# Graph layers on one core: x by V formed ahead of its signs, an identity product ahead of w, stores in another order

## The reference

```
L0: h = relu(batchnorm((A_hat x) W1' + b1)); out = batchnorm(h W2' + b2)
L1: L_norm = D^-1/2 (D - adj) D^-1/2;  _, U = eigh(L_norm)
    agg = U' x;  h = relu(agg W1 + b1);  out = U (h W2 + b2)
L2: graph attention over 256 edges, 4 heads, softmax by source node
L3: two graph convolutions, then LSTMs over windows of 1, 2, 3, 4 nodes
```

## Time and profile before

| | |
|---|---|
| median of 3 runs | 983.21 us (983.03 to 986.38) |
| profiled execution, its time | 983.05 us |
| its span in the trace | 981.2 us |
| TensorE busy | 900.8 us, 92%, 4041 matmuls |
| VectorE busy | 609.9 us, 62% |
| ScalarE busy | 609.8 us, 62% |
| GpSimd busy | 162.3 us, 17% |
| chain that ended last | PE 71%, DVE 16%, ACT 8%, issue 3% |

### The profile page before, as it was taken

How to read it: one execution, slowest core, us unless ns; L and a number is a source line. 1 busy time by engine, 2 the same in 40 slices (tenths; PEclk the granted TensorE clock), 3 DMA queues, 4 the chain that set the end, 5 groups by cost and what they waited for, 6 DMA issues and landing times.

```text
span 981.2 us, 13503 instructions
## 1 busy us (share of the span) xinstructions
PE 900.8 (92%) x4041; PEld 577.1 (59%) x4041; DVE 609.9 (62%) x2143; ACT 609.8 (62%) x1540; POOL 162.3 (17%) x458
## 2 busy tenths in 40 slices
PE   6999968788789987999999999999999999999994
PEld 4565555455566655677776777874444566644442
DVE  6677766657678864666468984335444444444686
ACT  4656647747368862686553456349767788865556
POOL 2334334324333330000000000000000000000065
PEclk9999969979789997999999999999999999999998
DMA  9200000000000000000000000000000000000014
GB/s 268 56 1 1 1 2 1 1 1 2 0 2 1 1 1 1 1 1 1 1 1 1 1 1 1 1 1 1 1 0 1 0 1 1 0 1 0 1 43 129
DMA packets 14329, 13.01 MB, mean 13 GB/s; under 512 B 896, under 2 KB 11056, under 8 KB 14256
## 3 DMA queue, kind: packets, MB, share of 16 engines
q1 hardware_dynamic: 14018, 11.98, 4.4%
q10 hardware_dynamic: 238, 0.16, 0.1%
HBM read 7.89 MB, written 4.19 MB: 12 GB/s over the span
## 4 chain that ended last, share of the span: by engine, by line
PE 71%; DVE 16%; ACT 8%; issue 3%; POOL 1%; DMA 0%; DVEq 0%; ACTq 0%; POOLq 0%
PE bank L982 18%; PE bank L1006 9%; PE bank L844 3%; PE bank L901 3%; PE bank L891 3%; PE bank L834 2%; PE bank L645 2%; PE bank L644 2%; PE bank L573 2%; PE bank L525 2%; PE bank L809 2%; PE bank L969 2%; PE bank L909 2%; PE bank L961 2%; PE bank L798 1%
## 5 line engine op out<-in xcount | busy, mean ns | idle before, releaser
L1489 ACT ACTIVATE hid_t<-bank,gate_b 128x512 f32<-128x512 f32 (+1 forms) x252 | 149.1, 632 | 48.8 <-PE bank L1006 48.2
L1600 POOL TENSOR_SCALAR x<-x,perm 128x128 f32<-128x128 f32 x32 | 29.4, 933 | 575.8 <-DVE perm L2240 575.8
L1006 PE MATMUL bank<-ms,w_t 128*128 128x512 f32 (+1 forms) x288 | 110.8, 528 | 0.1
L982 PE MATMUL bank<-hid_t,w_t 128*128 128x336 f32 (+1 forms) x296 | 106.6, 506 | 1.2 <-DVE x L2215 1.2
L982 PE MATMUL bank<-feat_t,w_t 128*128 128x512 f32 x208 | 93.1, 603 | 0.0
L982 PEld LDWEIGHTS bank<-hid_t,w_t 128*128 128x128 f32 x296 | 55.8, 190 | 46.3 <-issue 25.8
L1006 PEld LDWEIGHTS bank<-ms,w_t 128*128 128x128 f32 x288 | 54.1, 190 | 48.1 <-issue 33.8
L982 PEld LDWEIGHTS bank<-feat_t,w_t 128*128 128x128 f32 x208 | 39.1, 189 | 51.0 <-issue 46.5
L1496 ACT ACTIVATE hid_t<-hid_t 128x512 f32<-128x512 f32 (+1 forms) x72 | 41.8, 581 | 34.8 <-DVE hid_t L2199 25.6
L1276 ACT ACTIVATE pair<-bank,con 128x1 f32<-128x1 f32 x62 | 16.2, 262 | 72.9 <-PE bank L645 72.5
L1085 ACT ACTIVATE x<-x,perm 128x128 f32<-128x128 f32 x128 | 52.3, 482 | 2.6 <-DVE perm L1632 2.6
(11 more groups left out here) (427 smaller groups left out, 2061.6 us busy)
## 6 DMA issues: line engine op xcount, KB each, us to landing
out<-x SPq DMA_DIRECT2D x16, 256.0 KB, 2.6
con<-in_constants SPq DMA_DIRECT2D x1, 449.5 KB, 3.2
feat_t<-in_L_gnn_W SPq DMA_DIRECT2D x2, 128.0 KB, 3.6
e_int<-in_L_gnn_src ACTq DMA_DIRECT2D x1, 128.0 KB
l_w<-in_L_gnn_W SPq DMA_DIRECT2D x2, 64.0 KB
wg<-in_L_gnn_Wg SPq DMA_DIRECT2D x2, 64.0 KB
adj_n<-in_adj SPq DMA_DIRECT2D x1, 64.0 KB, 3.3
x<-in_x SPq DMA_DIRECT2D x4, 0.5 KB, 9.8
```

Of the source, the lines that this page charges most:

```text
L982: return mm(bank[4 * u + BANK_OF[g]][:, 0:w], w_t[:, WB_IH + 4 * (it.p - 1) + g, :], lstm_x(n), start=True, stop=(it.k == 0))
L1006: mm(bank[4 * u + BANK_OF[g]][:, 0:w], w_t[:, WB_HH + 4 * (it.p - 1) + g, :], lstm_h_of(it.chain)[:, 0:w], start=False, stop=True).then_in ...
L1489: f(dst[:, 0:w], bank[4 * u + BANK_OF[g]][:, 0:w], ACT.Tanh if g == G_G else ACT.Sigmoid, bias=gate_b[:, 4 * (it.p - 1) + g:4 * (it.p - 1) ...
L1600: d = pool.tensor_scalar(x[:, t * TB + b, :], x[:, t * TB + b, :], fin_mv[:, t, b, 0:1], fin_rs[:, t, b:b + 1], ALU.subtract, ALU.mult)
```

## The change

Six edits:

- `pe_rows`: weights of 128 columns of a wider `pair` where 33 were. `pe_rank`: pv and w have rows of their own (`two`); identity by A is a product ahead of the wait for w, with the group left open, and behind the wait stand pv by w and w by pv. Fillers that fall into an open group accumulate.
- Layer 1's aggregation is x by V (`v_nat`, without signs): tile t of 16 is formed by `l1_ahead(t)`, tiles 0 and 1 where fillers were, 2 to 7 behind the six levels, 8 to 15 within `eigen_signs`. ScalarE copies each to `feat_t` (`l1_ahead_kept`).
- Signs: TensorE multiplies ones by the diagonal of signs and gives them as a row; VectorE multiplies tiles 0 and 1 by it, GpSimd tiles 2 to 15, in place. Then u_t. The transpose and u_nat go.
- Layer 1's turn: mid, hidden of turn j+1, y. ScalarE's `fetched` goes.
- `edge_rest` and `head_rows` are split: the sums go to `removal_turn`, the head strips between the levels, the masks (`soft_masks`) to turn 3 of layer 2.
- The end: tile 11 goes to GpSimd, tile 14 to ScalarE, and SP stores in the order `FIN_ORDER`.

```diff
-FIN_POOL, FIN_ACT, FIN_DVE = range(8), (8, 9, 10, 11, 12, 13), (15, 14)
+FIN_POOL, FIN_ACT, FIN_DVE = (0, 1, 2, 3, 4, 5, 6, 7, 11), (8, 9, 10, 12, 13, 14), (15,)
+FIN_ORDER = (0, 1, 2, 3, 4, 5, 8, 6, 9, 10, 7, 12, 13, 11, 15, 14)
...
-        pair, pv_ident = sb("pair", [P, P]), sb("pv_ident", [P, P])
+        pair, two = sb("pair", [P, 3 * P]), sb("two", [1, 2, P])
...
-            for t, name, count in done:
+            for t, name, count in sorted(done, key=lambda d: FIN_ORDER.index(d[0])):
...
-                    filled(384, slot == HALF - 1)
-                    filled(128, slot == HALF - 1)
+                    filled(384, slot == HALF - 1, slot not in (STEPS_BEFORE - 1, HALF - 1))
+                    filled(128, slot == HALF - 1, slot not in (STEPS_BEFORE - 1, HALF - 1))
...
-                mm(h_both[:, k:P], pair[:, h:h + HALF + 1:2], a_sb[:, k:P], start=True, stop=True).then_inc(s["h_rows"], 1)
+                mm(bank[5][:, k:P], pair[:, h:h + 2 * P - 1:2], a_sb[:, k:P], start=True, stop=True).then_inc(s["h_rows"], 1)
+                if h != STEPS_BEFORE - 1:
+                    mm(h_mat[:, k:P], ident, a_sb[:, k:P], start=True, stop=False)
 
             def pe_rank(h):
                 if h is None or h in (STEPS_BEFORE - 1, HALF - 1):
                     return
                 k = h + 1
                 pe.wait_ge(s["h_w"], h + 1)
-                mm(h_mat[:, k:P], ident_pv, a_sb[:, k:P], start=True, stop=False)
+                mm(h_mat[:, k:P], pv, w_row[:, k:P], start=False, stop=False)
                 mm(h_mat[:, k:P], w_row, pv[:, k:P], start=False, stop=True).then_inc(s["h_rank"], 1)
...
-                filled(384, False)
-                filled(384, False)
+                l1_ahead(0)
                 pe_kept_turned(HALF, 1)
-                filled(128, False)
+                l1_ahead(1)
                 pe_kept_products(HALF, 1)
                 for level in range(6):
                     pe_solve(HALF, 5, level, 6)
+                    l1_ahead(2 + level)
                 pe_basis(HALF, 11)
                 pe.wait_ge(s["e_signs"], 3)
                 mm(pa[0][:, 0:3], ones[0:1, :], hs[0:1, 18:21], start=True, stop=True).then_inc(s["basis_pe"], 1)
 
+            def l1_ahead(t):
+                if t == 0:
+                    pe.wait_ge(s["x_ready"], CREDIT + TILES)
+                    pe.wait_ge(s["j_v_sb"], SWEEPS + 1)
+                if t > 3:
+                    pe.wait_ge(s["l1_agg_sb"], t - 3)
+                for b in range(TB):
+                    d = mm(l0_last[t % 4][:, b * P:(b + 1) * P], x[:, t * TB + b, :], v_nat, start=True, stop=True)
+                d.then_inc(s["l1_agg"], 1)
+
             def eigen_signs():
+                l1_ahead(8)
                 pe.wait_ge(s["signs_dve"], 1)
                 mm(pa[1][:, 0:2 * len(SPLITS) + 1], v_nat, q_cols[:, :], start=True, stop=True).then_inc(s["basis_pe"], 1)
-                for _ in range(2):
-                    kept_busy()
+                for t in range(9, ROW_AFTER):
+                    l1_ahead(t)
                 pe.wait_ge(s["signs_dve"], 2)
-                tr(ph[0][:, 0:P], u_t[:, :], ident).then_inc(s["basis_pe"], 1)
+                mm(pa[0][:, P:2 * P], ones[:, :], sign_mat, start=True, stop=True).then_inc(s["basis_pe"], 1)
+                for t in range(ROW_AFTER, TILES):
+                    l1_ahead(t)
 
             def layer1():
-                pe.wait_ge(s["signs_dve"], 3)
                 pe.wait_ge(s["small_loaded"], 16 * 7)
 
-                def early(j):
-                    for u in range(2):
-                        if j:
-                            pe.wait_ge(s["l1_agg_sb"], 2 * j + u - 1)
-                        for b in range(TB):
-                            t = mm(pa[u][:, b * P:(b + 1) * P], x[:, (2 * j + u) * TB + b, :], u_nat[:, :],
-                                   start=True, stop=True)
-                        t.then_inc(s["l1_agg"], 1)
-
-                def work(j, next_early):
-                    for u in range(2):
-                        pe.wait_ge(s["l1_agg_sb"], 2 * j + u + 1)
-                        mm(ph[u][:, :], l1_w1[:, :], at[u][:, :, :], start=True, stop=True).then_inc(s["l1_hid"], 1)
+                def hidden(t):
+                    if t < SIGNED_DVE:
+                        pe.wait_ge(s["signs_dve"], SIGNED_ROW + t + 1)
+                    else:
+                        pe.wait_ge(s["l1_pool"], t - SIGNED_DVE + 1)
+                    if t < 2:
+                        pe.wait_ge(s["l1_agg_sb"], TILES - 3 + t)
+                    mm(ph[t % 2][:, :], l1_w1[:, :], feat_t[:, t * TB:(t + 1) * TB, :], start=True, stop=True).then_inc(s["l1_hid"], 1)
+
+                def work(j, next_hidden):
                     for u in range(2):
                         pe.wait_ge(s["l1_hid_sb"], 2 * j + u + 1)
+                        if j == 0 and u == 0:
+                            pe.wait_ge(s["l1_agg_sb"], TILES - 1)
                         for b in range(TB):
                             t = mm(pm[u][:, b * P:(b + 1) * P], ht[u][:, b, :], l1_w2[:, :], start=True, stop=True)
                         t.then_inc(s["l1_mid"], 1)
-                    next_early()
+                    next_hidden()
+                    if j == 0:
+                        pe.wait_ge(s["signs_dve"], SIGNED_T)
+                        pe.wait_ge(s["l1_agg_sb"], TILES)
                     for u in range(2):
                         pe.wait_ge(s["l1_mid_sb"], 2 * j + u + 1)
                         pe.wait_ge(s["l1_added"], CREDIT + 2 * j + u - 1)
                         mm(py[u][:, :], u_t[:, :], ms[u][:, :, :], start=True, stop=True).then_inc(s["l1_y"], 1)
 
-                pe.wait_ge(s["x_ready"], CREDIT + 16)
-                ahead_written_out(PAIRS, early, work)
+                ahead_written_out(PAIRS, lambda j: (hidden(2 * j), hidden(2 * j + 1)), work)
...
+                l1_ahead_kept(0)
                 act_kept_turned(1)
+                l1_ahead_kept(1)
                 for level in range(5):
                     act_solve(HALF, 1, level)
+                    l1_ahead_kept(2 + level)
+                for t in range(7, TILES):
+                    l1_ahead_kept(t)
+
+            def l1_ahead_kept(t):
+                act.wait_ge(s["l1_agg"], t + 1)
+                f(feat_t[:, t * TB:(t + 1) * TB, :], l0_last[t % 4][:, :], ACT.Copy).then_inc(s["l1_agg_sb"], 1)
...
-                    if j + 1 < PAIRS:
-                        fetched(2 * j + 2)
-                        fetched(2 * j + 3)
...
-                for t in (11, 12):
+                for t in (12, 13):
                     final_normalised(t)
                 final_root(4)
-                final_normalised(13)
+                final_normalised(14)
...
+            pool.wait_ge(s["signs_dve"], SIGNED_ROW)
+            for t in range(SIGNED_DVE, TILES):
+                pool.wait_ge(s["l1_agg_sb"], t + 1)
+                tile = feat_t[:, t * TB:(t + 1) * TB, :]
+                pool.tensor_tensor(tile, tile, s_row.unsqueeze(1).broadcast_to([P, TB, P]), ALU.mult).then_inc(s["l1_pool"], 1)
...
+            def head_strips(h):
+                if h == 0:
+                    link(dve.memset(head_strip, 0.0))
+                if h < HEADS:
+                    link(copy(head_strip[h * DH:(h + 1) * DH, P - HEADS + h:P - HEADS + h + 1], v_cols[h * DH:(h + 1) * DH, VR_A:VR_A + 1]))
...
+                edge_sums()
...
+                ts(sign_mat, ident, COL(11), None, ALU.mult).then_inc(s["signs_dve"], 1)
+                dve.wait_ge(s["basis_pe"], AT_BACK)
+                copy(s_row, pa[0][:, P:2 * P]).then_inc(s["signs_dve"], 1)
+                dve.wait_ge(s["signs_dve"], SIGNED_ROW)
+                for t in range(SIGNED_DVE):
+                    l1_signed(t)
                 ts(u_t[:, :], v_t, COL(11), None, ALU.mult).then_inc(s["signs_dve"], 1)
-                dve.wait_ge(s["basis_pe"], AT_BACK)
-                copy(u_nat[:, :], ph[0][:, 0:P]).then_inc(s["signs_dve"], 1)
+
+            def l1_signed(t):
+                dve.wait_ge(s["l1_agg_sb"], t + 1)
+                tile = feat_t[:, t * TB:(t + 1) * TB, :]
+                tt(tile, tile, s_row.unsqueeze(1).broadcast_to([P, TB, P]), ALU.mult).then_inc(s["signs_dve"], 1)
...
+                    if t == 3:
+                        soft_masks()
```

More of the change, by code:

```diff
@@ L292, in graph_layers @@
         vp_row.insert(2, rows[:, 0:2, :])
[L293 to L294 removed]
+        a_sb, z_row, e_vec, a_row = u_t, s_flt[0:1, :], rows[:, 2, :], (rows[:, 3, :], rows[:, 4, :])
+        pv, w_row = two[:, 0, :], two[:, 1, :]
         def c_col(h):
@@ L568, in behind_rank, with filled @@
                     l0_hidden(slot - A_HID0, 0)
-            def filled(cols, rows_read):
+            def filled(cols, rows_read, opened=False):
                 into = bank[5] if rows_read else bank[6]
-                mm(into[:, P:P + cols], ident, con[:, 0:cols], start=True, stop=True)
```

(8 more changed lines are left out.)

35 lines of the change are left out of this document (15 added, 20 removed).

## The result

| | before | after |
|---|---|---|
| median | 984.65 us, 4 runs (983.03 to 986.38) | 972.43 us, 4 runs (970.96 to 974.34) |
| profiled execution, span | 983.05, 981.2 us | 971.44, 969.6 us |

The ratio is 0.9884, 95% interval 0.9861 to 0.9907: faster by 12.2 us, where 10.6 were forecast. (Before has one run more here than ahead of the prediction.)

What follows compares the result with a forecast made beforehand. Eigensolver turns and solve were taken as bound by latency, the layers by TensorE's throughput; -7.7 + 1.0 + 3.0 - 5.4 - 1.5 = -10.6 from 983.05 gave 972.4, stated as 972.5 us; forecast 968 to 978, range 962 to 982.

Steps and rivals of the forecast that it cites:

- Layer 1 loop: Layer 1's turns lose the aggregation; ScalarE's root before the next relu then holds them at 6.2 us: gain 7.7 us.
- Start of layer 1: Before layer 1's first second-weight product: aggregations of tiles 12 to 15 don't hide; cost 1.0 us (-0.5 to +2.5).
- I expect the solve to end where it ends now: Last solve: tiles 2 to 7 behind its levels, 1.4 us each at full clock, leave its end unchanged.
- Steps of the turns: Eigensolver steps: wider row product and identity by A add 21 us of TensorE load, mostly absorbed; cost 3 us (0 to 21).
- the chain from w to the next column keeps its length: Eigensolver steps: two products still follow w, and a 1-row weight load takes 0.184 us like a full one.
- Clock: Eigensolver turns: added products keep TensorE's clock up, curing 15 of 64 us at 1.2 GHz; gain 5.4 us (0 to 23).
- The prediction's 0.36: Eigensolver turns: each us at half clock costs 0.36 us; a 3.4 us stretch costs 1.22 us.
- Tail: End of the kernel: stores issued as tiles come, not queued behind GpSimd's tile 7; gain 1.5 us (0.5 to 2.5).
- GpSimd: Layer 1: sign products for 14 tiles, taken at 1.8 us each, hidden up to 3.1 us each.
- Rival C: Layer 1: GpSimd at 3.5 us a tile ends 5.5 us late, 978 us, or VectorE is held; chance 0.10.
- A: Rival: root doesn't hold layer 1's turn (another 4.8 us), or most low clock goes (14.4 us); 962 to 968 us, chance 0.22.
- B: Rival: the steps' 21 us load lands on the eigensolver's path, 995.9 us; chance of slower 0.08, of no change 0.10.

Runs made afterwards that it cites:

- padding: Changed kernel with pv and w's tile made 128 rows high with zeros, both rank products reading 128 rows: 963.12 us, ratio 0.9781.
- the filled solve: Kernel before with a 128x256 product into a free bank behind each of the last solve's six levels: 981.67 us, ratio 0.9972.
- the moved root: Changed kernel with layer 1's root of pair j-1 moved on ScalarE from before the relus of turn j+1 to behind them: 968.39 us, ratio 0.9840.

## Why the prediction was right, step by step

**Layer 1 loop, -7.7: -8.06.** The mechanism and the place of it as written. That the root holds the turn is shown by moving it: 5.2 to 5.3 us.

**Start of layer 1, +1.0: +2.43.** The tiles 12 to 15 were sized well: from the diagonal of signs (before: from u_t) to the first second-weight product it is 6.05 us instead of 4.95, +1.1. The step that failed is "I expect the solve to end where it ends now". The first level comes 0.72 us later behind the last V product (tile 0 waits for V, which the filler products in its place didn't, and two tiles are longer than they were), the five levels take 1.68 us each, +0.70 in sum, though the low clock has gone from them, and the last basis another 0.33; the sign chain got 0.4 back. I had a level at 0.5 + 0.89 = 1.4: in the rows the aggregation holds 1.09 us behind 64-row weights, since their change of size costs there as well, and the three products 0.59.

**Steps of the turns, +3.0: a gain, not a cost.** This is the term with the wrong sign. The prediction counted the wider row product as weight load alone (107 to 184 ns). Those durations were right, but the product behind narrow weights had been starting late, and in turns 1 to 3 that went: -0.4 us a turn, against +0.1 for the rest. The sentence "the chain from w to the next column keeps its length" rested on the same durations; the 0.14 and 0.28 us gained in turns 7 and 10 by the new order are where it failed, and padding takes another 0.3 us off a turn.

**Clock, -5.4.** Both factors were too large. Of the 64 us in the turns 15 were to go, and 6.8 went; the other 13.7 of the 20.5 us lie in the solve and the sign chain, where the aggregations took up what the clock gave. Each was worth 0.17 to 0.27 us in most places that the experiments compare, and 0.36 in one turn. The prediction's 0.36 came from two steps with different work of TensorE in them: 5.07 us from 216.50, and 6.29 us from 286.92. Between the starts of the same two updates lie 6.12 us in the timeline of before and 5.44 where the clock is full (287.11 in the trace with the filled solve): 0.20 for each. The prediction also has the fall of the clock at 287.08; it came at 289.12, and from 287.08 to then TensorE was busy without a break (2.04 of 2.04 us in the window of before, at a grant of 1.00).

So 6.8 us x 0.25 = 1.7, and 2.4 at 0.36, not 5.4. The total of the turns is -3.66. The seven at full clock in both traces (0 to 3, 6, 7 and 10) give -2.4 of it, 0.8 in turn 0 and 0.14 to 0.32 in the others. The nine that have low clock in one trace or both give the rest, some shorter (0.8 us in turns 12 and 14, whose low clock went), some longer: the removal turn takes 0.58 us more, and turn 15, with 10.2 us at the low clock instead of 3.4, takes 2.4 more. Which turns are hit can't be told ahead from these traces; the same edit moved them about in each kernel.

**Tail, -1.5: -2.1 alone.** The order of events was the forecast one, and the term a little small.

**GpSimd.** A sign product takes 1.27 us, and 1.77 and 1.72 in the first two, beside VectorE's (taken: 1.8). No product of TensorE waits for one. Rival C's held VectorE is real, but not as the prediction had it: it looked for operations with two SBUF inputs and excluded the statistics. What was stretched on the path was a 128x8 tensor_scalar with one input, which the prediction took to be free of GpSimd, and behind it the 128x8 scalar_tensor_tensor (L1659) of the scale, which has two inputs in SBUF and was overlooked. The Trainium skill (SBUF — State Buffer, "SBUF: two separate sides") does name VectorE operations in a 2-port mode beside those with two inputs, and says that the one that starts first has the port for a whole instruction. The runs agree that VectorE waits; a hold of 3.20 us over products of 1.27 is longer than one instruction, and ends with the run of them.

So the mechanism of the largest term was right, and that the sum came out within 2 us was in part luck, with two terms wrong in opposite ways: 3.0 - 5.4 = -2.4 was forecast for the turns and -3.66 came, for another reason. The start of layer 1, short by 1.4 us, cancelled against that. Rivals A and B didn't come about; A's condition (no root) is worth 4 us, and the moved root gives 968.4, just above A's range of 962 to 968.

## What to carry to other kernels

Between small products that stand in a chain, look at how far apart the starts are, not at durations, and whether each weight load starts before its product; where weights change in rows or columns from one product to the next, try padding with zeros to one size. A late start costs only where no wait stands behind it: look at more than one turn before a gain is put down to it. When an aggregation or any other work leaves a loop, read from the trace which wait stood second in it, and move that too. Keep GpSimd's runs of SBUF products away from VectorE's small operations on a critical ring, or break them up.

## What was unexpected of the hardware

A 33-column or 1-row set of weights between 128x128 ones costs about 0.1 us at each change where TensorE has work queued (0.31 to 0.40 against 0.22 us from start to start); with 64-row weights the aggregation behind takes 1.09 us against 0.95. Where TensorE waits soon after, nothing of it is left: turn 7 is 18.34 us with 128 columns and 18.33 with 33. Products that nobody reads made a turn shorter: 20.12 to 16.67 us, with the clock at 0.97 instead of 0.63 in it. And a 128x8 operation of VectorE lasted 3.20 us beside GpSimd in one kernel and 3.17 in another, and 0.17 without. Why a change of size keeps the load from starting early is open: the traces show only that it does.
